# Causal attention without mask matmuls: GpSimd zeroes the future keys; in the other attentions GpSimd adds the queries

## What is computed

```python
x = x + _L0_xattn_ref(_layernorm(x), ctx_1024, ctx_1024, ...)      # phase A0
x = x + _L0_ffn_ref(_layernorm(x), ...)                            # F0
x = x + _L1_xattn_ref(_layernorm(x), ctx_1024, ...)                # A1
x = x + _L1_ffn_ref(_layernorm(x), ...)                            # F1
x = x + _L2_xattn_ref(_layernorm(x), ctx_1024, ctx_1024, ..., mask_1x1xSxS2_ik0)   # A2
x = x + _L2_ffn_ref(_layernorm(x), ...)                            # AS, then F2
x = x + _L3_xattn_ref(ctx_1024, ctx_1024, _layernorm(x), mask_Bx1x1xS2_if1, ...)   # A3
x = x + _L3_ffn_ref(_layernorm(x), ...)                            # F3

# the causal attention inside _L2_ffn_ref:
scores = jnp.einsum('bqhd,bkhd->bhqk', q, k)
mask = jnp.arange(t)[:, None] < jnp.arange(t)[None, :]
scores = jnp.where(mask, -jnp.inf, scores)
attn = jax.nn.softmax(scores / np.sqrt(HEAD_DIM), axis=-1)
```

## Time and profile before

| | us |
|---|---|
| median of 3 runs (lowest, highest) | 1829.16 (1824.91, 1830.92) |
| the profiled execution's own time | 1826.0 |
| its span in the profile | 1824.2 |

### The profile page before, as it was taken

The page is one execution under the profiler, slowest core; times in us unless marked ns, Lnnn a source line. Parts: engine busy times, 40 slices in busy tenths (PEclk is TensorE's granted clock), DMA queues, the critical chain, the costliest instruction groups (busy, mean ns, idle before and its releaser), DMA issues.

```text
span 1824.2 us, 38603 instructions
## 1 busy us (share of the span) xinstructions
PE 1710.1 (94%) x14287; PEld 1154.1 (63%) x14322; DVE 1177.5 (65%) x3559; ACT 1031.1 (57%) x2018; POOL 596.1 (33%) x1173
## 2 busy tenths in 40 slices
PE   6999988999999999989999999989998999999998
PEld 3555546455559888854444455558885555589997
DVE  5898958889852332357878676646657888733332
ACT  2777752677774444436666654443334777744442
POOL 4344332333222122313333344323352444222221
PEclk7999988899999999979999999989998999999999
DMA  5444202445300000312323145300031543100000
GB/s 164 123 134 145 75 24 76 132 137 165 112 3 7 1 1 1 93 52 82 119 77 101 45 125 145 89 1 1 1 103 61 178 147 118 34 1 7 7 7 7
DMA packets 114853, 132.36 MB, mean 73 GB/s; under 512 B 14934, under 2 KB 78700, under 8 KB 114668
## 3 DMA queue, kind: packets, MB, share of 16 engines
q1 hardware_dynamic: 114668, 129.90, 23.6%
HBM read 83.45 MB, written 46.40 MB: 71 GB/s over the span
## 4 chain that ended last, share of the span: by engine, by line
PE 79%; DVE 11%; ACT 4%; issue 3%; DMA 1%; POOL 1%; SPq 0%; DVEq 0%; POOLq 0%; ACTq 0%
PE ps_s L1391 16%; PE ps_av L1247 14%; PE ps_s L1205 12%; PE ps_t L1367 10%; DVE mx L1683 6%; PE ps_t L1220 4%; PE ps_s L1367 4%; PE ps_t L1231 3%; ACT prob L970 3%; PE ps_m L1303 2%; PE ps_m L1288 2%; PE ps_m L1294 2%; DVE qmx L1692 2%; PE ps_m L1281 1%; PE ps_m L1316 1%
## 5 line engine op out<-in xcount | busy, mean ns | idle before, releaser
L970 ACT ACTIVATE prob<-ps_t 128x512 f32<-128x512 f32 (+1 forms) x1152 | 615.5, 585 | 290.8 <-PE ps_t L1220 290.3
L1683 DVE TENSOR_REDUCE mx<-ps_s 128x1 f32<-128x512 f32 x752 | 479.7, 683 | 57.3 <-PE ps_s L1205 53.0
L1205 PE MATMUL ps_s<-kst,qst 32*128 32x512 f32 (+2 forms) x1248 | 381.8, 481 | 34.3 <-DVE mx L1683 19.3
L1391 PE MATMUL ps_s<-w_ffn,prob 128*128 128x128 f32 x2688 | 322.8, 277 | 0.0
L1391 PEld LDWEIGHTS ps_s<-w_ffn,prob 128*128 128x128 f32 x2688 | 316.1, 193 | 10.3 <-issue 3.4
L1220 PE MATMUL ps_t<-qmx,kst 32*128 32x256 f32 (+1 forms) x2304 | 315.7, 335 | 3.5 <-ACT prob L970 3.5
L1205 PEld LDWEIGHTS ps_s<-kst,qst 32*128 32x128 f32 x1248 | 162.8, 189 | 232.6 <-issue 92.3
L1247 PE MATMUL ps_av<-prob,vaug 128*32 128x256 f32 (+1 forms) x4608 | 306.9, 385 | 3.2 <-ACT avs L1011 3.2
L1978 DVE SCALAR_TENSOR_TENSOR acc<-ps_s,comb,acc 128x128 f32<-128x128 f32 x336 | 94.6, 344 | 256.7 <-PE ps_s L1391 256.7
L1143 ACT ACTIVATE prob<-ps_t,b1c 128x512 f32<-128x512 f32 x204 | 125.4, 686 | 238.2 <-PE ps_t L1367 238.2
L1220 PEld LDWEIGHTS ps_t<-qmx,kst 32*128 32x128 f32 x2304 | 193.8, 188 | 16.8 <-ACT prob L970 13.3
(11 more groups left out here) (241 smaller groups left out, 2256.6 us busy)
## 6 DMA issues: line engine op xcount, KB each, us to landing
kst<-k_parts SPq DMA_DIRECT2D x128, 256.0 KB, 3.6
qst<-q_parts SPq DMA_DIRECT2D x160, 128.0 KB, 3.8
k_parts<-k_hi SPq DMA_DIRECT2D x64, 256.0 KB, 3.0
q_parts<-q_hi SPq DMA_DIRECT2D x80, 128.0 KB, 2.4
ctxT<-in_ctxT SPq DMA_DIRECT2D x32, 256.0 KB, 2.7
k_parts<-k_lo SPq DMA_DIRECT2D x32, 256.0 KB, 3.3
q_parts<-q_lo SPq DMA_DIRECT2D x40, 128.0 KB, 2.4
w_ffn<-in_F_w SPq DMA_DIRECT2D x18, 256.0 KB, 2.9
```

The lines of the kernel that those rows point to most:

```text
L970: nc.scalar.activation(row[:, S * kt:S * kt + w], ps_t[TURN[unit(ph, g, n) % 8]][:, 0:w], ACT.Exp).then_inc(sig["exp_done"], 1)
L1205: pe.matmul(dst, qst[p][strip, g, q * 128:(q + 1) * 128], kst[p][strip, g, 0:nk], start=True, stop=True).then_inc(sig["s_ready"], 1)
L1391: mm = pe.matmul(dst, h[:, c, 128 * q:128 * (q + 1)], w2c, start=(c == 0 and not bias), stop=(c == nc_h - 1))
L1683: dve.tensor_reduce(mx[:, buf, i:i + 1], src, AX.X, ALU.max, negate=True).then_inc(sig["max_done"], 1)
```

## The change

- AS has no mask matmuls. Its transposed scores open their bank themselves and wait for the exponential that last used it. The tile caus_T goes.
- POOL sets the probabilities of future keys to zero instead: `cut_future`, one affine_select for each unit, over the two diagonal blocks of 128 x 128 in prob, after the unit's exponential. `values` in AS waits for `cut_done` of the group before.
- AS has its units 2 and 3 in quarter 2, not 3, and the values of the group before (both key tiles) in quarter 2, not 1.
- In A0, A1, A2 and A3 the maxima no longer go from ps_m to qmx by one DVE instruction. ACT copies ps_m into the new tile mturn (in the slot MT, in its queue behind the exponential of that half), which gives ps_m free; POOL adds mturn and the queries into qmx; the transposed scores wait for POOL's `mq_done`. AS keeps the DVE instruction, now called `add_queries`.
- The maxima are split into two bfloat16 parts, not three: two POOL instructions a group, not four, in all phases.

```diff
@@ POOL
+            def add_queries(ph, bt, g):
+
+                wait(pool, "mt_read", cnt.at("mt_read", ph, bt, g))
+                pool.tensor_tensor(qmx[:, g % 2, :], mturn[:, :], qst[bt.parity][:, g, :].bitcast(F32), ALU.add).then_inc(sig["mq_done"], 1)
+
+            def cut_future(bt, g, n):
+
+                wait(pool, "exp_done", cnt.at("exp_done", "AS", bt, unit("AS", g, n)))
+                diagonal = prob[:, g % 2, HEAD_T[n], 0:2 * S].rearrange("p (c s) -> p c s", c=2)[:, :, 0:128]
+                pool.affine_select(out=diagonal, in_=diagonal, compare_op=ALU.is_ge, fill=0.0, base=0, pattern=[[0, 2], [1, 128]],
+                                   channel_multiplier=-1).then_inc(sig["cut_done"], 1)
...
                 link(pool.tensor_copy(part[0], neg))
-                link(pool.tensor_tensor(rest, neg, part[0], ALU.subtract))
-                link(pool.tensor_copy(part[1], rest))
-                pool.tensor_tensor(part[2], rest, part[1], ALU.subtract).then_inc(sig["msplit"], 1)
+                pool.tensor_tensor(part[1], neg, part[0], ALU.subtract).then_inc(sig["msplit"], 1)
@@ ACT
+            def maxima_T(ph, bt, g):
+                wait(act, "mt_ready", cnt.at("mt_ready", ph, bt, g))
+                wait(act, "mq_done", cnt.at("mq_done", ph, bt, g) - 1)
+                nc.scalar.activation(mturn[:, :], ps_m[:, 0:S], ACT.Copy).then_inc(sig["mt_read"], 1)
@@ PE
-                p, opened = bt.parity, ATT[ph]["mask"] in ('full', 'causal')
+                p, opened = bt.parity, ATT[ph]["mask"] == "full"
...
-                    wait(pe, "mt_read", cnt.at("mt_read", ph, bt, g))
+                    done = "mt_read" if ph == "AS" else "mq_done"
+                    wait(pe, done, cnt.at(done, ph, bt, g))
...
-            return {0: 0, 3: 2}[k] + half if k in (0, 3) else None
+            return {0: 0, 2: 2}[k] + half if k in (0, 2) else None
```

More of the change, by code:

```diff
@@ L824, in body @@
                         ahead = unit_after(ph, bt, last, g, 2)
+                        nxt = unit_after(ph, bt, last, g, 1)
+                        adds = nxt[0] and nxt[0] != "AS"
                         if ph == "A0" and (bt.b, g) in ((0, 1), (0, 3), (1, 1)):
@@ L1243, in values @@
                         wait(pe, "v_read", cnt.at("v_read", ph, bt))
[L1244 removed]
+                done = "cut_done" if ph == "AS" else "exp_done"
+                wait(pe, done, cnt.at(done, ph, bt, unit(ph, g, HG * (kt // 2) + HG - 1)))
                 buf = g % 2
```

71 lines of the change are left out of this document (42 added, 29 removed).

## The result

The changed kernel takes 1861.01 us (median; 1853.88 to 1867.89) against 1829.18 us, a ratio of 1.019 with a 95% interval of 1.0155 to 1.0225: 32 us slower by the medians, where 16 us faster was forecast. A ratio in this document is a measured one, taken over the executions within 1.5% of the fastest of their kernel, and not the quotient of the two medians. The profiled execution of the changed kernel took 1867.9 us, the longest of its four, with a span of 1866.2, 42.0 us over the span of before.

| stretch | before | after | difference |
|---|---|---|---|
| start, A0 | 239.2 | 235.4 | −3.8 |
| F0 | 80.8 | 81.8 | +1.0 |
| A1 | 201.8 | 196.8 | −5.0 |
| F1 | 265.4 | 268.2 | +2.8 |
| A2 and the edge to AS | 256.8 | 258.1 | +1.3 |

What follows compares the result with a forecast made beforehand. TensorE, 94% busy, was taken as the bound, with DVE also near it in A0, A1, A3. Masks −13, query part −4, A2 0, phase edges −1, clock +2 gave −16: 1829.16 to 1813 us; 8-in-10 range 1796 to 1831.

Steps and rivals of the forecast that it cites:

- The clock, +2 us: AS: with fewer matmuls and longer waits on PE, TensorE's granted clock drops somewhat more, costing 2 us.
- the query part: A0, A1, A3: ACT copies and POOL adds queries in place of DVE; −0.17 us a batch, −4 us over 24 batches.
- Rival 2: AS: the clock eats the gain, 0.80 in place of 0.95, +18 us, total about 1829, no change; chance 0.15.
- The masks, −3.25 us a batch with 1.5 given back: AS: removing 16 mask matmuls saves 3.25 us a batch; 1.5 returns as quarter 3's waits for DVE; −13 us overall.
- The strips' DMA: AS: the 8.6 us from POOL's k_hi to PE's first reader does not shrink, so part of the masks' gain returns.
- The selects: AS: 16 selects a batch on POOL, 0.41 to 0.73 us each, fit and cost nothing unless POOL lags a group.
- The two tiny instructions less a group: POOL, splitting the maxima into two parts, not three: 256 tiny instructions fewer, zero effect.
- "0.2" for a DVE that is ahead: A1, group 0: the scores' weight load waited 0.35 us for a maximum; DVE 0.4 ahead gives about half, 0.2.
- Rival 4: A0, A1, A3: DVE was the real bound; −16 to −27 us in 24 batches, total 1790 to 1801; chance 0.12.
- A2: Attention A2: same query edit, but DVE is idle 6 us a batch; zero, between −2 and +3 us.
- Rival 1: ACT's copies queue behind exponentials and free ps_m late: +32 us, total about 1846, slower; chance 0.10.

## Why the prediction failed, step by step

**The clock, +2 us: the step that failed.** I read the earlier trace rows as a slope (7% fewer matmuls for 0.09 of clock) and asked how far it would go on. It is a step between two levels, and what grows is the time at the lower one: in the old quarters the longest low stretch is 10 us with the 16 masks a batch (17 with the query part too), 68 with 8, 171 and 177 with none, and at 0.50 PE is 95% busy for batch after batch. Measured: +39.2 us in AS, and a part of F2's 7.7, since its first 14 us are at the low clock too, in place of +2. Rival 2 named the mechanism, gave it 0.15 and priced it with the same slope: 0.80 and +18 us, where 0.55 and +39 came. The row to ask was not how much the clock had sunk but that it sank at all with PE 94% busy, and the edit took 128 matmuls out of that stage. Why the low level lasts without them, and why the same number in other places did not bring the clock back as well, stays open; the busy share explains neither. The Trainium skill's rule in TensorE: Matmul & The Clock Gate, section What's actually happening (throttled by default, activity releases it) gives the direction of this loss and not its size. The runs agree with the direction, 190.4 us of AS without the masks against 161.5 with unused matmuls in their places. But a PE that this profile shows 95% busy stayed at 0.50, so activity as a busy share would not have told it. The prediction's own sign for rival 2, a clock in AS below 0.85, came with 0.55.

**The masks, −3.25 us a batch with 1.5 given back.** At an equal clock the old quarters without masks gave 1.45 us in the first batch, where I had 2.0 (1.3 in a batch held by the DMA). For the new quarters there is no whole batch at 1.00. The changed kernel's first three groups of AS took 6.80, 2.80 and 5.26 us against 6.95, 4.26 and 5.27 before, 1.6 us less, all at 1.00. As far as they go the size was about right. It was paid out only until the clock fell.

**The strips' DMA.** Not tested: at the low clock the waits for it are gone, and no kernel without masks kept the high one long enough.

**The selects.** 0.41 us each, free: right, also at the full clock, where a batch with the selects and unused matmuls takes 19.63 us, as before. At 0.73 us they would not have fitted, as the prediction says they would: 8.52 and 11.7 are over 19.60. The two tiny instructions less a group are 320 in five attentions (POOL's 1173 instructions become 1107 with 128 selects and 128 adds more and two of the setup less), not 256; the zero put on them is not tested apart.

**The query part, −0.17 a batch: undersized.** Both waits that I read moved as I said, 0.58 gained in group 3 (I had 0.55) and 0.33 lost in group 1 (0.45). But the term that mattered was the smallest I wrote, "0.2" for a DVE that is ahead: measured 1.50. The chain put 16.9% on DVE's maxima; PE's weight loads waited for them eight times in the batch, 3.2 us in all, and of the 1.68 us taken from DVE nine tenths count. Rival 4 had that mechanism, with 1.13 less 0.45 at its lower end; it was 1.50 less 0.70, and its sign, A1 batches under 25.5, came with 25.45. It had the wrong total too: steady batches of A0 and A3 gain less than those of A1, and a part is given back at the phases' ends, A1 −5.0 but F1 +2.8, A3 −3.6 but F3 +2.4. How much of that is the query part's is uncertain by half: in the profiles of kernels without it F1 takes 265.2 to 266.9 us and F3 237.5 to 239.1, and in nearly all with it 268.2 or more and 240 (266.9 and 238.5 the least). In the last group of A1 and A3, where PE has no plain scores to do, the clock of the changed kernel drops once: the sixteen values' matmuls at the end of A1 take 1.57 us in the changed kernel (first row, timeline of PE), and 1.07 in the kernel before (second row).

```profile
522.75 1.57 PE L1285 MATMUL ps_av<-prob,vaug 128*32 128x256 f32 x16
```

```profile
530.44 1.07 PE L1247 MATMUL ps_av<-prob,vaug 128*32 128x256 f32 x16
```

Such a drop is not the query part's alone: the kernel before with one unused matmul a group has one behind A3, and that with the mask matmuls left out one behind A1. Four more matmuls there took nothing away in A3, and in A1 it isn't shown that they did; the rest of the 2.4 to 2.8 us (ACT's last copy is 0.4) stays open. Net, the whole query part is worth 4 us by the medians and nothing by the ratio. That is close to the −4 of the sum, but by luck: the gain in a steady batch was over four times as large, and what is given back was not in the sum.

**A2**, zero: right, 30.81 us a batch in both. **Rival 1** (ACT's copies late, slower) did not happen; the sign came from another cause.

## What to carry to other kernels

Before taking work off TensorE, look at the granted clock of that stage, not at its busy share: if it already leaves 1.00 there, the work that seems wasted may be what holds the rest at full speed, and the price of losing it can be nearly the whole stage at half the clock, not a share of it. When a stage turns slow after such an edit, put unused matmuls of the same size in the same places; that one run tells the missing work from whatever else the edit did. Put them in the same places: elsewhere the same number brought back less, or did harm. And where an engine that is not the busiest (DVE, 89%) has the busiest one waiting for it again and again, eight times in this batch, count what you take from it nearly in full.

## What the runs showed of the hardware

- TensorE, busy for 95% of a batch, stayed at 0.50 for nearly 200 us but for one short rise, while the same stage with 16 mask matmuls a batch more was 93% busy over its first 89 us, all at 1.00. The granted clock could not be read from the busy share.
- Such a stage fell to 0.50 with the masks too. What differed most was how long it stayed there: 10 us at the most in the kernel before and 17 with masks and the query part, 68 with half the masks, 171 and 177 with none. The new quarters with masks had one of 72.
- The same code ran at either level in one execution: batches of 20.0 and of 30.8 us.
- The same 16 unused matmuls a batch gave a mean clock of 0.94 in the masks' places (in the old order), 0.79 at the heads of quarters 1 and 3 (in the new order), and 0.54 between the strips' matmuls, where they also undo the overlap of four 32-row matmuls.
- POOL's affine_select costs 0.41 us for 128x256 both in bf16 and in f32 from strided blocks, while its add of two tensors of that size in f32 costs 0.73.
